# AdaLN and quantised feed-forward kernel: the fourth pair of samples 4 to 6 from high and low parts, earlier splits for the guest, 48 transposes before the last selection

## What is computed

```python
h  = einsum('bij,bkj->bik', x, cond_weight[ids])         # a matrix per sample
h  = layernorm(h) * gamma + beta
h  = fake_quant(h) @ fake_quant(w1).T + b1               # int8 grid
h  = fake_quant(gelu(h)) @ fake_quant(w3).T + b3
x1 = x + h
y  = x1 @ weight.T + bias + scale * (x1 @ a.T) @ b.T     # the base matrix and a low-rank part
heads = rmsnorm(y) @ W.T + base                          # 4x4 logits, two 4-vectors
H  = (1 - g) * I + g * sinkhorn(heads / tau, 50 rounds)  # per token, 4x4
out = x1 + H @ streams(y) + post * ((pre . streams(y)) @ W_branch)
```

## Time and profile before

| | us |
|---|---|
| median of 3 runs | 791.6 (790.79 to 793.91) |
| the profiled execution | 791.53 |
| its span, first to last instruction | 789.7 |

### The profile page before, as it was taken

One profiled execution on the slowest core, in us unless ns is written; L12 is line 12 of the kernel. 1 busy time (PEld: TensorE's weight loads), 2 busy tenths in 40 slices (PEclk: granted clock), 3 DMA queues, 4 the chain that ended last, 5 costly groups with the idle time before them and its releaser, 6 DMA issues.

```text
span 789.7 us, 10179 instructions
## 1 busy us (share of the span) xinstructions
PE 727.0 (92%) x3228; PEld 490.2 (62%) x3228; DVE 555.2 (70%) x1933; ACT 374.2 (47%) x682; POOL 68.0 (9%) x40
## 2 busy tenths in 40 slices
PE   9989999999999999989998999998999994799937
PEld 6555444364656666434765788887878773567626
DVE  4558675537888887782865513517898988999985
ACT  2253735316556454543543643436324342699614
POOL 0002000200202022533031000000000000000000
PEclk9999999999999999999999999999999998799969
DMA  7959974243555542826032203113032157665406
GB/s 297 411 171 405 268 271 150 81 161 98 187 182 187 187 173 81 310 76 227 27 134 92 99 26 120 55 67 118 5 120 71 52 170 251 216 216 184 138 0 213
DMA packets 54279, 124.32 MB, mean 157 GB/s; under 512 B 8015, under 2 KB 33743, under 8 KB 48722
## 3 DMA queue, kind: packets, MB, share of 16 engines
q1 hardware_dynamic: 52930, 120.94, 44.1%
q10 hardware_dynamic: 1296, 2.74, 0.9%
HBM read 98.47 MB, written 25.19 MB: 157 GB/s over the span
## 4 chain that ended last, share of the span: by engine, by line
PE 52%; DVE 20%; ACT 10%; DMA 10%; issue 5%; SPq 2%; POOL 1%; ACTq 0%; DVEq 0%
PE PS L1080 15%; PE PS L969 10%; PE PS L905 8%; DMA stage<-w_dram 4%; PE PS L894 4%; DMA wscale_scratch<-wsc 3%; PE PS L958 2%; PE PS L1232 2%; PE PS L1192 2%; PE PS L1002 2%; DVE xp L1494 2%; DMA out_dram<-mr 2%; ACT blk L834 2%; DVE hbuf L1293 2%; PE PS L1186 2%
## 5 line engine op out<-in xcount | busy, mean ns | idle before, releaser
L905 PE MATMUL PS<-w_raw,x_raw 128*128 128x512 f32 x336 | 150.0, 600 | 4.7 <-DMA x_raw<-x_tr_dram 3.4
L905 PEld LDWEIGHTS PS<-w_raw,x_raw 128*128 128x128 f32 x336 | 63.1, 193 | 76.8 <-issue 73.2
L1080 PE MATMUL PS<-w_hi,xT_hi 128*128 128x512 f32 x256 | 103.3, 404 | 0.0
L1080 PE MATMUL PS<-w_hi,xT_lo 128*128 128x512 f32 x256 | 100.5, 393 | 0.0
L1080 PE MATMUL PS<-w_lo,xT_hi 128*128 128x512 f32 x256 | 100.3, 392 | 0.0
L514 POOL TENSOR_TENSOR xres<-xres,vecs 128x1024 f32<-128x1024 f32 x16 | 42.8, 2696 | 311.5 <-DMA xres<-x_tok_dram 311.5
L1399 DVE TENSOR_TENSOR xT_lo<-PS,xT_hi 128x512 fp32r<-128x512 f32 x32 | 20.6, 682 | 66.0 <-ACT xT_hi L662 65.8
L1588 DVE TENSOR_REDUCE ksum<-kprod 128x16 f32<-128x64 f32 x392 | 66.1, 209 | 0.0
L595 ACT ACTIVATE qT<-PS,round_c 128x512 bf16<-128x512 f32 x64 | 40.1, 678 | 45.7 <-PE PS L958 45.6
L969 PE MATMUL PS<-w3q,qT 128*128 128x512 bf16 x256 | 58.0, 379 | 1.0 <-ACT qT L595 1.0
L969 PE MATMUL PS<-w1q,qT 128*128 128x512 bf16 x256 | 57.9, 379 | 0.8 <-ACT qT L595 0.7
(11 more groups left out here) (190 smaller groups left out, 1393.8 us busy)
## 6 DMA issues: line engine op xcount, KB each, us to landing
w_raw<-cond_w_dram SPq DMA_DIRECT2D x31, 1024.0 KB, 5.7
x_raw<-x_tr_dram SPq DMA_DIRECT2D x32, 256.0 KB, 6.4
stage<-w_dram SPq DMA_DIRECT2D x16, 512.0 KB, 12.1
xres<-x_tok_dram SPq DMA_DIRECT2D x8, 1024.0 KB, 8.3
x_scratch<-x1buf SPq DMA_DIRECT2D x16, 512.0 KB, 5.1
x1n<-x_scratch SPq DMA_DIRECT2D x16, 512.0 KB, 6.1
y_scratch<-y SPq DMA_DIRECT2D x16, 512.0 KB, 3.1
stage<-base_w_nat_dram SPq DMA_DIRECT2D x8, 512.0 KB, 12.5
```

The source lines that it names most:

```text
L905: mm = pe.matmul(PS[:, 2 * t + h, :], x_raw[pr][:, c, t * P:(t + 1) * P], w_raw[pr][:, c, h * H2:(h + 1) * H2], start=(pr == 0 and c == 0) ...
L1080: pe.matmul(PS[:, 2 * t + h, :], xx[:, c, t * P:(t + 1) * P], ws[c // 2][:, c % 2, h * H2:(h + 1) * H2], start=(c == 0 and xx is xT_hi and ...
```

## The change

Pair 3 of samples 4 to 6 is parted too: its high parts are made on ACT behind `quant1(s-1, 1)`, its low parts on DVE ahead of `finish_w3(s-2, 1)`. The guest's split 2 moves on ACT from step 7 to step 6, split 3 to an earlier place in step 7, and POOL does split 2 ahead of `add_b3(5)`. The stores of the head matrices go to the start of SP's step 4 and the wait for them to where the bias rows are loaded. Before `select(1)` PE issues 48 transposes of the identity, once only three Sinkhorn rounds are left. The last tile is added and stored in two halves.

```diff
--- before.py
+++ after.py
@@ -40,7 +40,7 @@
     HG = GROUP // 2
     MIX = 4
     GUEST = NB - 1
-    FIRST = (3, 3, 4, NB)
+    FIRST = (3, 3, 4, 4)
     TQ = P // NS
     SEL_BANK = 4
     BLK = 3
@@ -257,6 +257,8 @@
         K_OPS = 6
         SK_OPS = 12
         B_ITERS = 12
+        K0 = 3 + K_OPS * (SINKHORN - 1) + 1
+        WARM_ITERS, WARM_LAST = 3, 48
 
 
         @block.sync
@@ -383,15 +385,18 @@
                 load_w(s + 1, 2)
                 load_w(s + 1, 3)
 
+            def store_heads():
+                sp.wait_ge(c_sb, 2)
+                sp.dma_start(c_dram.rearrange("a r n -> (a r) n"), csb[:, 0, :]).then_inc(c_st, 16)
+                sp.dma_start(cb_dram, csb[0:1, 1, :]).then_inc(c_st, 16)
+
             for s in range(2, NB - 1):
+                if s == 4:
+                    store_heads()
                 if s + 1 == GUEST:
                     step_a_base(s)
                 else:
                     step_a(s)
-            sp.wait_ge(c_sb, 2)
-            sp.dma_start(c_dram.rearrange("a r n -> (a r) n"), csb[:, 0, :]).then_inc(c_st, 16)
-            sp.dma_start(cb_dram, csb[0:1, 1, :]).then_inc(c_st, 16)
-            sp.wait_ge(c_st, 32)
             def load_x1n(b, t):
                 sp.wait_ge(x1_st[t], b * 16 + 16)
                 wait(sp, xt_done, b * 4 + (2 * t - 2))
@@ -435,6 +440,7 @@
                 load_x1n(1, t)
 
             sp.wait_ge(b_set, 1)
+            sp.wait_ge(c_st, 32)
...
@@ -488,12 +494,15 @@
...
-            for i in range(GROUP):
+            for i in range(GROUP - 1):
                 sp.wait_ge(f_add, i + 1)
                 sp.dma_start(streams(out[GROUP + i]), nr[i][:, :, :]).then_inc(n_st, 16)
+            for h in range(2):
+                sp.wait_ge(f_add, GROUP + h)
+                sp.dma_start(streams(out[NT - 1])[:, 2 * h:2 * h + 2, :], nr[GROUP - 1][:, 2 * h:2 * h + 2, :]).then_inc(n_st, 16)
             for i in range(MIX):
                 sp.wait_ge(o_st[i], GROUP // MIX * 16)
-            sp.wait_ge(n_st, 16 * GROUP)
+            sp.wait_ge(n_st, 16 * (GROUP + 1))
 
 
         @block.gpsimd
@@ -518,8 +527,8 @@
                 add_b3(s)
             split_lo(0)
             split_lo(1)
+            split_lo(2)
             add_b3(GUEST - 2)
-            split_lo(2)
             split_lo(3)
             for s in range(GUEST - 1, NB):
                 add_b3(s)
@@ -667,15 +676,14 @@
                     ln_root(s - 1, 0)
                 quant1(s - 1, 0)
                 pair_high(s, 2)
-                if s == GUEST:
-                    split_hi(2)
                 if s == 3:
                     composites_2()
                 evac_T(s - 2, 1, 3)
+                if s == GUEST:
+                    split_hi(3)
                 ln_root(s - 1, 1)
                 quant1(s - 1, 1)
-                if s == GUEST:
-                    split_hi(3)
+                pair_high(s, 3)
                 evac_T(s - 1, 0, 1)
                 pair_high(s + 1, 0)
                 pair_high(s + 1, 1)
@@ -701,6 +709,8 @@
                     evac_T(s - 1, 0, 3)
                     return
                 evac_T(s - 1, 0, 3)
+                if s == GUEST - 1:
+                    split_hi(2)
                 gelu(s - 1, 1)
                 ln_root(s, 0)
                 quant2(s - 1, 1)
@@ -1231,7 +1241,15 @@
                 for j in range(NS):
                     mm = pe.matmul(region(i, j), last_blk(i)[:, j, :, :].rearrange("p t q -> p (t q)"), ny[i][:, j, :],
                                    start=True, stop=True)
-                mm.then_inc(fm_done, 1)
+                    if j == NS - 1 or (i == GROUP - 1 and j == 1):
+                        mm.then_inc(fm_done, 1)
+
+            def keep_warm():
+
+                pe.wait_ge(hs_step, 2)
+                pe.wait_ge(k_step[0], K0 + 3 + K_OPS * (SINKHORN - 1 - WARM_ITERS))
+                for i in range(WARM_LAST):
+                    pe.transpose(PS[:, SEL_BANK + i // 4 % 2, (i % 4) * P:(i % 4 + 1) * P], ident[:, :], ident[:, :])
 
             select(0)
             for i in range(AHEAD):
@@ -1248,6 +1266,7 @@
             for i in range(AHEAD, GROUP):
                 pe.wait_ge(nx_ld[i], 16)
                 rest_part(GROUP + i, GROUP + i, nr[i], True)
+            keep_warm()
             select(1)
             for i in range(GROUP):
                 last(i)
@@ -1417,6 +1436,7 @@
                 finish_w3(s - 2, 0)
                 pair_low(s, 2)
                 layer_norm(s - 1, 1)
+                pair_low(s, 3)
                 finish_w3(s - 2, 1)
                 pair_low(s + 1, 0)
                 pair_low(s + 1, 1)
@@ -1573,8 +1593,6 @@
                     nc.vector.memset(kb[i][:, :, :], 1.0).then_inc(k_step[i], 1)
 
 
-            K0 = 3 + K_OPS * (SINKHORN - 1) + 1
-
             def half(k, row):
 
                 vec, new = (kb, ka) if row else (ka, kb)
@@ -1682,6 +1700,13 @@
 
             def last_add(i):
 
+                if i == GROUP - 1:
+                    for h in range(2):
+                        dve.wait_ge(fm_done, GROUP + h)
+                        nc.vector.tensor_tensor(nr[i][:, 2 * h:2 * h + 2, :].rearrange("p j c -> p (j c)"),
+                                                PS[:, 2 * (i % 2) + h, :],
+                                                nr[i][:, 2 * h:2 * h + 2, :].rearrange("p j c -> p (j c)"), ALU.add).then_inc(f_add, 1)
+                    return
                 dve.wait_ge(fm_done, i + 1)
                 nc.vector.tensor_tensor(nr[i][:, :, :].rearrange("p (b j) c -> p b (j c)", b=2),
                                         PS[:, 2 * (i % 2):2 * (i % 2) + 2, :],
```

## The result

| | before | after |
|---|---|---|
| median | 792.75 us (4 runs) | 804.32 us (4 runs, 803.94 to 806.42) |
| profiled execution | 791.53 | 804.48 |
| its span | 789.7 | 802.7 |

The ratio is 1.015, with a 95% interval of 1.0115 to 1.0186: slower, by 11.6 us in the medians. The forecast was 800 us, its range 794 to 804, so the time lies just above the range. The median of the kernel before had been 791.6 us with three runs; the fourth moved it to 792.75.

A forecast was written before the change was run, and what follows sets the result against it. It took PE, ACT and DVE to take turns in one loop of about 41.5 us in steps 4 to 6, and loads to bound the guest's step. +15.3 - 6.0 - 0.6 = +8.7 on 791.53 gave 800.2, forecast 800 us, range 794 to 804.

The forecast's parts named there:

- The rival in which the conversions hide: Steps 4 to 6: ACT and DVE absorb the new work in idle times; 779 us in all, chance 0.08.
- clock term: Steps 4 to 6: PE's low clock after each new idle gap loses 1.7 us per gap.
- part 2: Steps 4 to 6: cost of pair 3's conversions in the loop, +15.3 us with the cheaper pair already taken off.
- upper end of 2.2: Steps 4 to 6: most lost per gap to the low clock, half of 4.4 us; gives 5.7 per sample.
- the path: Steps 4 to 6: delay of the loop without clock loss, 3.4 us per sample, 3 x 3.4 = 10.2.
- the upper bound, 3 x 5.7: Steps 4 to 6: three samples, each 5.7 us late if 2.2 us are lost to the clock.
- the 3.4 per step: Steps 4 to 6: lower bound of the delay per sample, with nothing lost to the clock.
- DVE's own path: Step 4: 3.72 + 2.81 - 2.19 = 4.3 us late, so l0(5, 0) starts 4.3 us later.
- The guest: Guest's step: waits of 3.42 and 1.74 and a clock loss of 1.80 go, less 1.0 new; -6.0 us.
- what is late next: Guest's step: POOL's block of splits delays DVE ahead of quant2(5, 1), 1.0 us, between nothing and 2.0.
- The end: Last stage: transposes gain nothing, the halved last tile saves 0.6; -0.6 us, between -2.3 and +0.5.
- The rival in which transposes don't raise the clock: Last selection: 48 transposes stay at 0.20 us each, selection 3.4 us late and slow; 804 us, chance 0.06.

The follow-up runs named there:

- e2: The kernel before with only pair 3 of samples 4 to 6 made from high and low parts: 810.55 us, ratio 1.023.
- e1: The changed kernel with pair 3 of samples 4 to 6 multiplied as fp32 again, all else kept: 785.67 us; repeated, 785.63 us.
- e3: The changed kernel with pair 3's high parts one place later on ACT and its low parts one place later on DVE: 794.46 us, ratio 1.0009.
- e4: The changed kernel with 22 small fp32 matmuls adding zeros in PE's gaps of steps 4 to 6: 798.24 us, ratio 1.0072.
- e5: The kernel before with the guest's earlier splits on ACT and POOL alone: 788.08 us, ratio 0.9936.
- e6: The kernel before with only the head stores and the wait for them moved: 792.21 us, ratio 1.0000.
- e7: The changed kernel without pair 3's parts and without the 48 transposes: 787.89 us, ratio 0.9941 to the kernel before.
- e9: As e1, with ACT's split 2 behind ln_root(6, 0), so POOL subtracts after DVE's centring: 786.41 us, ratio 0.9906.

## Why the prediction came out as it did

**The mechanism was right, in its place and its order.** The bank, freed by `finish_w3`, ended PE's wait (5.12 us for 5.1 said); DVE waited 3.63 us (3.72 said); the wait of 2.19 us was gone. e2 has the gaps without the rest of the change, e1 the rest without the gaps, and e3 removes them by the place alone. The rival in which the conversions hide fell: DVE's idle times were not where its new work was put.

**The step that failed is the size of the clock term in part 2.** I took 1.7 us per gap, 5.1 in all, and 3.4 us at the low level behind each, from a case in which the fall came 0.9 us after PE had resumed. Even the upper end of 2.2 assumed that PE would need no longer to get its clock back than it did there (4.4 us as I read it, 4.3 by finer rows). Here the clock fell in the gap and stayed down until 4.5, 5.3 and 5.7 us after PE had resumed: the products took 2.20, 2.58 and 2.76 us more than 3.63, 7.5 in all, two of them above that upper end. The steps grew by 17.1 us instead of 15.3. Without the products' 7.5 the path took 9.6 for the 10.2 said. So the clock term was 2.4 us too small, the path 0.6 too large, and that the sum stayed at the upper bound, 3 x 5.7, is partly luck.

With the clock held (e4) the steps were 11.1 longer for the 10.2 said. Steps 5 and 6, 3.5 and 3.3 longer, bear out the 3.4 per step. Step 4 was 4.3 longer: with PE on time it was DVE's own path, the 4.3 of the prediction, that came last there (PE waits 0.51 us for ACT at its end). The prediction had this path for `l0(5, 0)` but left it out of its lower bound.

**The guest** saved 5.0 instead of 6.0: the waits went as said, and the term "what is late next" was too small, too: 1.47 us ahead of the transposes of (5, 1) plus 0.25 and 0.23 at two other places, about 2.0 for 1.0 said, which was its upper end. Where I had costed the move of the head stores as giving the 1.74 us, e5 shows the earlier split did it alone, and e6 that the stores alone gave under a microsecond.

DVE's share in this can be read in e1: POOL's subtraction ended at 333.92 and DVE's instruction, begun at 330.87, ended at 335.01, 1.1 us later, where its like alone takes 1.28 us in all. The Trainium skill (SBUF — State Buffer, "Who interferes with whom") has the second instruction of such a pair wait for the whole of the first. By that, the traces agree.

**The end** came out at -1.0 for -0.6 said, because the halved tile saved more: from the first of the last products to the last addition 0.5 us, and 0.4 from there to the end of the span. As said, the transposes overran (by 1.2 us), the selection took 1.06 instead of 2.06, and the clock fell again in or behind the gap of 2.4 us. So in this execution they gained next to nothing, as said: 0.1 us from the rounds to the first product. As a statement on the kernel it was too low: by the medians of e7 they are worth some 2 us, though no single comparison there is clear of the scatter. The nearest row, 15.70, came from one execution, and this time differs from one to the next. The price of 0.20 for a transpose at the low level came from a row whose first half microsecond was still at the full clock; it did no harm, the 48 took 7.17 us for 7.4 said.

The rival in which transposes don't raise the clock is refuted: from 772.00 PE did nothing but transposes, at clock 0.50, and at 776 it was 1.00. The Trainium skill (TensorE: Matmul & The Clock Gate, Part 4) says that the full clock doesn't engage for transposes. By that, the traces disagree, and for these transposes the measurement decides.

**Where the 4.1 us between 800.2 and 804.32 come from.** 1.2 us are the time of the kernel before, 791.53 in the forecast's sum and 792.75 in the median of four runs. The other 2.9 are the change: the steps cost 1.8 more and the guest saved 1.0 less. The end gave 0.4 back; the rest is within the scatter of the runs. With either of the first two at its size as said, the time would have been within the range, which it left by 0.3 us.

## What to carry to other kernels

When three engines hand two tiles round in one loop, cost new work by the place in each queue, not by the engine's share: work that needs another engine's answer before it, put ahead of what frees a bank, costs its wait and its length, and removing 1.3 us of matmul is no match for it. Of the 17 us lost here 6 were the amount of work, 5 its place, and 6 the clock: a gap of 5 us in PE cost another 2 us behind it. If a stretch must be idle, small matmuls in it pay back, but they should end before the wait does.

## What the runs showed that I had not expected

The low clock was still there after 4.5 to 5.7 us of work where it had fallen within a gap, and for 4.3 us where it fell just after one. Gaps of 2.4 us ahead of the last products were followed by either level in two executions of the same kernel (14.08 and 15.63 us). And DVE's wait for POOL could not be saved by shifting POOL's instruction a little: in e9 the same POOL work cost the same path 1.6 us at the next instruction instead of 1.45 at the first.
